# Attention and gated FFN on one core: small steps of the down product moved ahead of the attention's steps in each queue, one operand pair regrouped, bias, weight forms and loads at other places

## The reference

```python
x = x + attn(layernorm(x), ...)   # latent attention, causal, RoPE, width 64 after two projections
x = x + ffn(layernorm(x), W1, W2, W3)
# ffn: hidden = silu(x @ W1.T) * (x @ W3.T)      hidden width 2048
#      hidden = fwht(hidden)                     Walsh-Hadamard transform over 2048
#      out    = hidden @ W2.T
# attn: c = (x @ W_to_kv.T) @ W_compress.T; layernorm; q, k, v from c; RoPE; softmax(q k / 8) v;
#       z = o @ W_comp2lat.T; out = z @ W_to_kv + z @ W_out_res.T + b_out_res
```

## Time and profile before

| what | value |
|---|---|
| three runs, median (lowest to highest) | 2144.19 us (2143.27 to 2144.85) |
| the profiled execution's own time | 2144.14 us |
| its span in the trace | 2142.1 us |
| PE / DVE / ACT / POOL busy | 2010.1 / 1525.1 / 1157.8 / 1066.0 us |
| instructions | 32782 |

### The profile page before, as it was taken

How to read it: one execution, slowest core, us unless ns; L and a number is a source line. 1 busy time by engine, 2 the same in 40 slices (tenths; PEclk the granted TensorE clock), 3 DMA queues, 4 the chain that set the end, 5 groups by cost and what they waited for, 6 DMA issues and landing times.

```text
span 2142.1 us, 32782 instructions
## 1 busy us (share of the span) xinstructions
PE 2010.1 (94%) x11862; PEld 1167.0 (54%) x11862; DVE 1525.1 (71%) x2626; ACT 1157.8 (54%) x1775; POOL 1066.0 (50%) x788
## 2 busy tenths in 40 slices
PE   6889899989999999999999999999999999999998
PEld 3534344455555656556555555556565555556665
DVE  7897978758777686776777677776768768653333
ACT  5866455455554655555555646556564555543343
POOL 2356732556356454554546544554644545454444
PEclk8999999999999999999999999999999999999999
DMA  8656346454463524735346434545347353373322
GB/s 328 222 193 228 123 143 164 153 156 138 121 155 125 188 88 142 173 108 164 115 116 171 148 123 123 138 138 163 113 126 178 100 163 113 100 168 125 119 96 89
DMA packets 267264, 312.57 MB, mean 146 GB/s; under 512 B 181344, under 2 KB 191712, under 8 KB 265312
## 3 DMA queue, kind: packets, MB, share of 16 engines
q1 hardware_dynamic: 267104, 310.48, 47.7%
HBM read 221.02 MB, written 47.19 MB: 125 GB/s over the span
## 4 chain that ended last, share of the span: by engine, by line
PE 52%; DVE 19%; ACT 10%; issue 9%; POOL 6%; DMA 3%; SPq 1%; ACTq 0%; DVEq 0%; POOLq 0%
PE PF L1115 10%; PE PF L1117 10%; PE PF L1116 10%; PE PD L1199 4%; PE PD L1200 4%; PE PD L1201 4%; DVE H L2240 2%; POOL ring L2502 2%; DVE XS L2208 2%; DMA WS<-wscr 1%; DVE W2S L2234 1%; DVE Pl L1987 1%; ACT H L1593 1%; PE XY L936 1%; ACT W2S L1572 1%
## 5 line engine op out<-in xcount | busy, mean ns | idle before, releaser
L1115 PE MATMUL PF<-XF,WS 128*128 128x512 f16 x1778 | 676.2, 380 | 25.8 <-ACT PF L1545 10.3
L1116 PE MATMUL PF<-XF,WS 128*128 128x512 f16 x1778 | 674.3, 379 | 0.0
L1117 PE MATMUL PF<-XF,WS 128*128 128x512 f16 x1778 | 674.1, 379 | 0.0
L1199 PE MATMUL PD<-W2S,H 128*128 128x256 f16 x1456 | 397.2, 273 | 33.5 <-ACT W2S L1601 14.8
L1201 PE MATMUL PD<-W2S,H 128*128 128x256 f16 x1456 | 397.1, 273 | 0.0
L1200 PE MATMUL PD<-W2S,H 128*128 128x256 f16 x1456 | 397.1, 273 | 0.0
L2572 POOL TENSOR_TENSOR ring<-ring,W2S 128x512 f32<-128x512 f32 x192 | 257.0, 1341 | 203.2 <-ACT W2S L1601 203.2
L1117 PEld LDWEIGHTS PF<-XF,WS 128*128 128x128 f16 x1778 | 174.0, 98 | 210.1 <-issue 0.7
L1115 PEld LDWEIGHTS PF<-XF,WS 128*128 128x128 f16 x1778 | 173.8, 98 | 193.0 <-issue 36.1
L2554 POOL TENSOR_TENSOR SH<-SH 128x512 f32<-128x512 f32 x112 | 162.2, 1448 | 196.0 <-DVE SH L2234 191.6
L1116 PEld LDWEIGHTS PF<-XF,WS 128*128 128x128 f16 x1778 | 174.3, 98 | 124.2 <-issue 4.8
(11 more groups left out here) (371 smaller groups left out, 3606.0 us busy)
## 6 DMA issues: line engine op xcount, KB each, us to landing
WS<-wscr SPq DMA_DIRECT2D x112, 896.0 KB, 4.9
W2S<-w2f SPq DMA_DIRECT2D x196, 256.0 KB, 2.7
ring<-x SPq DMA_DIRECT2D x56, 256.0 KB, 5.3
wscr<-WS SPq DMA_DIRECT2D x16, 896.0 KB, 4.2
out<-ring SPq DMA_DIRECT2D x56, 256.0 KB, 3.2
RAW<-w13t SPq DMA_DIRECT2D x16, 512.0 KB, 4.6
xraw<-xT SPq DMA_DIRECT2D x28, 256.0 KB, 4.1
XF<-w SPq DMA_DIRECT2D x13, 512.0 KB, 18.1
```

Of the source, the lines that this page charges most:

```text
L1115: pe.matmul(bank, wh, th, start=i < 2 and j == 0, stop=False, skip_group_check=True)
L1116: pe.matmul(bank, wh, tl, start=False, stop=False, skip_group_check=True)
L1117: m = pe.matmul(bank, wl, th, start=False, stop=j == 1, skip_group_check=True)
L1199: pe.matmul(o, th, wh, start=i in (P1, P2, P5) and tp == 0 and r == 0, stop=False, skip_group_check=True)
```

## The change

- `take_at` (ACT) and `add_at` (DVE) move one `fill` earlier: a unit that ends in step (k, j) is emptied ahead of `fill(k, j)` and no longer behind it. On DVE `fill(k, 5)` goes behind `hidden(k, 1)` and the addition, except where it holds a softmax low part (`low_at`).
- `SPLITS`: A12 is split alone (512 wide, ACT and DVE), early in the even block; A22 is split with S4 (1024 wide, ACT at the end of the even block, POOL at the head of the odd one). Their places and counts change with it, and DVE's `parts_low` loses a wait.
- `bias`: row t at slot `tile_slot(a, t) + 4`, with no wait for V.
- `TPREP`: two of W2's sums in stage 0 and six in stage 1 (four and four before), at other steps.
- cproj's first half is at slot 3 for a >= 3 (2 before); the load of WS for block 1 of a stage is at j = 1 (2 before), ahead of the load of form 6.

```diff
--- before.py
+++ after.py
@@ -73,15 +73,15 @@
 ADDED = (6, 7, 8, 9, 12, 13)
 HFORM = ("A11", "S2", "S3", "A22", "A12", "S1", "S4")
-PLACE_A = {"A11": (0, 0), "S3": (1, 8), "S1": (2, 3), "S2": (4, 4), "A12": (5, 6), "A22": (7, 7), "S4": (16, 17)}
-PLACE_B = {"A11": 9, "S3": 10, "S1": 11, "S2": 12, "A12": 13, "A22": 14, "S4": 15}
-
-SPLITS = (("A11", "S3"), ("S1", "S2"), ("A12", "A22"), ("S4",))
+PLACE_A = {"A11": (0, 0), "S3": (1, 8), "S1": (2, 3), "S2": (4, 4), "A12": (16, 17), "A22": (7, 7), "S4": (5, 6)}
+PLACE_B = {"A11": 9, "S3": 10, "S1": 11, "S2": 12, "A12": 15, "A22": 14, "S4": 13}
+
+SPLITS = (("A11", "S3"), ("S1", "S2"), ("A12",), ("S4", "A22"))
 SPLIT_OF = {f: i for i, fs in enumerate(SPLITS) for f in fs}
 WFILE = (4, 0, 1, 2, 5, 3, 6)
-TPREP = ({33: 0, 42: 1, 51: 2, 60: 3}, {8: 4, 22: 5, 36: 6, 50: 7})
+TPREP = ({48: 0, 59: 1}, {8: 2, 18: 3, 28: 4, 38: 5, 48: 6, 58: 7})
 SPLIT_AT = {13 + i: i for i in range(16)}
@@ -91,7 +91,7 @@
-FORMS_AT = {0: 2, 6: 2}
+FORMS_AT = {0: 1, 6: 2}
 SUMS_AT = 11
@@ -173,6 +173,12 @@
     return None if q < QF or q >= NK // 4 - 1 else (q, 7 * (k % 4) + j)
+def low_at(k, j):
+
+    s, h = divmod(k, NH)
+    return s > 0 and any(slot == tile_slot(c, t) + 2 for c, slot in slots(s, 7 * h + j) for t in range(4))
+
+
 def done_at(k, j):
     v = half_at(k, j - 1) if j else half_at(k - 1, 6)
@@ -199,12 +205,12 @@
 def high_no(p, i):
-    return 16 + 4 * (p - 2 * QF) + i + 1
+    return 16 + 4 * (p - 2 * QF) + {0: 1, 2: 2, 1: 3, 3: 4}[i]
 def low_no(p, i):
-    return 2 * (p - 2 * QF) + {0: 1, 3: 2, 1: 17, 2: 18}[i]
+    return 2 * (p - 2 * QF) + {0: 1, 3: 2, 2: 17, 1: 18}[i]
 def sum_no(p, i):
@@ -501,7 +507,7 @@
         def parts_from(p, i):
-            return (SH[:, :, :], SH[:, :, :], SHO[:, :, :], SHO[:, 0, :])[i]
+            return (SH[:, :, :], SH[:, :, :], SHO[:, 0, :], SHO[:, :, :])[i]
         def parts_free(p, i):
@@ -677,8 +683,8 @@
                 q, r = x // 2, x % 2
                 w.wait_ge(d_w2st[q % 2], 224)
-                if x in (0, 4):
-                    w.wait_ge(v_xf, xf_no(x // 4, 6))
+                if x in (0, 2):
+                    w.wait_ge(v_xf, xf_no(x // 2, 6))
                 else:
                     w.wait_ge(d_tst, 16 * x)
                 sp.dma_start(TP, w2scr[q][:, r * 2048:(r + 1) * 2048]).then_inc(d_tld, 16)
@@ -948,8 +954,8 @@
                 yfree = (v_x2, tile_no(a, t))
             def attention(a, slot):
-                if slot in (2, 5):
-                    for k in (0, 1) if slot == 2 else (2, 3):
+                if slot in (2 if a < PLAIN else 3, 5):
+                    for k in (2, 3) if slot == 5 else (0, 1):
                         if a < PLAIN:
                             cproj1(a, k)
                         else:
@@ -1780,57 +1786,55 @@
                     high(k - 1)
                 if k == 4 * QF + 4:
                     parts_high(k // 2 - 1, 0)
-                take_at(k, 0)
+                if k > 4 * QF + 1 and k % 2 == 0:
+                    parts_high(k // 2 - 1, 2)
+                take_at(k, 1)
                 fill(k, 0)
                 if k:
                     copy_p5(k)
                 if k == 1:
                     tokens_high(0, 6)
-                if k > 4 * QF + 2 and k % 2:
-                    parts_high((k - 3) // 2, 3)
-                take_at(k, 1)
+                take_at(k, 2)
                 fill(k, 1)
                 if k > 4 * QF + 1 and k % 2 == 0:
                     parts_high(k // 2 - 1, 1)
                 if k > 4 * QF and k % 2 and k != 4 * QF + 3:
                     parts_high(k // 2, 0)
-                take_at(k, 2)
-                if k > 4 * QF + 1 and k % 2 == 0:
-                    parts_high(k // 2 - 1, 2)
                 if split and k > 1:
                     forms_high(h + 1, 0)
                     forms_high(h + 1, 1)
+                take_at(k, 3)
                 fill(k, 2)
                 if k:
                     silu(k, 0)
-                take_at(k, 3)
+                take_at(k, 4)
                 fill(k, 3)
                 if k == 1:
                     forms_high(2, 0)
                     forms_high(2, 1)
-                take_at(k, 4)
+                take_at(k, 5)
                 fill(k, 4)
                 if k == 0:
                     norms(15, 0)
                 silu(k, 1)
-                take_at(k, 5)
+                take_at(k, 6)
                 fill(k, 5)
+                if k > 4 * QF + 1 and k % 2 == 0:
+                    parts_high(k // 2 - 1, 3)
                 if k == 0:
                     norms(15, 1)
                     norms(13, 0)
                     norms(13, 1)
                     tokens_high(0, 2)
                     norms(14, 0)
-                take_at(k, 6)
                 if k % 4 < 3:
                     fill(k, 6)
+            parts_high(NK // 2 - 1, 2)
             parts_high(NK // 2 - 1, 1)
             take(NK // 4 - 1, 0)
-            parts_high(NK // 2 - 1, 2)
             take(NK // 4 - 1, 1)
-            take(NK // 4 - 1, 2)
             parts_high(NK // 2 - 1, 3)
-            for u in COPIED[3:]:
+            for u in COPIED[2:]:
                 take(NK // 4 - 1, u)
@@ -2027,7 +2031,7 @@
                 w.wait_ge(v_xf, xf_no(a // 2 - 1, 6))
                 if a in (2, 4):
-                    w.wait_ge(d_tst, 32 * a)
+                    w.wait_ge(d_tst, 16 * (2, 8)[a // 2 - 1])
                 ve.tensor_scalar(XS[:, a % 2, t, :], xrow(a, t), st[:, 184 + 2 * t:185 + 2 * t], st[:, 84 + t:85 + t],
                                  ALU.subtract, ALU.mult).then_inc(v_xs, 1)
@@ -2236,7 +2240,6 @@
             def parts_low(p, i):
                 w.wait_ge(a_hi, high_no(p, i))
-                w.wait_ge(g_S, sum_no(p, 2))
                 ve.tensor_tensor(parts_at(p, i, 1), parts_from(p, i), parts_at(p, i, 0), ALU.subtract).then_inc(v_lo, 1)
             def add_unit(q, u):
@@ -2439,6 +2442,7 @@
                 s, h = divmod(k, NH)
                 if k > 1:
                     hidden(k - 1, 0)
+                    add_at(k, 0)
                     fill(k - 1, 6)
                 if k == 0:
                     hidden(0, 0)
@@ -2449,24 +2453,22 @@
                     tokens_low(0, 2)
                     tokens_low(0, 4)
                     tokens_sum(0, 6)
-                add_at(k, 0)
                 fill(k, 0)
                 if k and k <= 4 * QF:
                     low_part(k - 1)
-                add_at(k, 1)
+                if k > 4 * QF + 1 and k % 2 == 0:
+                    parts_low(k // 2 - 1, 2)
+                add_at(k, 2)
                 fill(k, 1)
                 if k:
                     sum_c(k)
                     out_rows((k - 1) // 4 - 1, 2 * ((k - 1) % 4) + 1)
                 if k > 4 * QF + 1 and k % 2 == 0:
                     parts_low(k // 2 - 1, 1)
-                add_at(k, 2)
                 fill(k, 2)
-                if k > 4 * QF + 1 and k % 2 == 0:
-                    parts_low(k // 2 - 1, 2)
                 if k and s == 0 and h < NH - 1:
                     forms_low(h + 1, 0)
-                add_at(k, 3)
+                add_at(k, 4)
                 fill(k, 3)
                 if k:
                     sum_e(k)
@@ -2474,19 +2476,21 @@
                     tokens_low(0, 6)
                 if k and s == 0 and h < NH - 1:
                     forms_low(h + 1, 1)
-                add_at(k, 4)
+                add_at(k, 5)
                 fill(k, 4)
                 out_rows(k // 4 - 1, 2 * (k % 4))
-                add_at(k, 5)
+                if low_at(k, 5):
+                    fill(k, 5)
                 hidden(k, 1)
-                fill(k, 5)
                 add_at(k, 6)
+                if not low_at(k, 5):
+                    fill(k, 5)
                 if k == 0:
                     fill(k, 6)
             hidden(NK - 1, 0)
             add_at(NK, 0)
+            parts_low(NK // 2 - 1, 2)
             parts_low(NK // 2 - 1, 1)
-            parts_low(NK // 2 - 1, 2)
             for u in ADDED:
                 add_unit(NK // 4 - 1, u)
@@ -2589,9 +2593,9 @@
                     row_add(*before)
                 if k > 4 * QF and k % 2:
                     if j == 0:
+                        if k > 4 * QF + 2:
+                            parts_low((k - 3) // 2, 3)
                         form_sum(k // 2, 0)
-                    if j == 1 and k > 4 * QF + 2:
-                        parts_low((k - 3) // 2, 3)
                     if j == 3 and k != 4 * QF + 3:
                         parts_low(k // 2, 0)
                 if k > 4 * QF + 1 and k % 2 == 0:
@@ -2600,14 +2604,13 @@
                             parts_low(k // 2 - 1, 0)
                         form_sum(k // 2 - 1, 1)
                         form_sum(k // 2 - 1, 2)
-                    if j == 3:
+                    if j == 2:
                         form_sum(k // 2 - 1, 3)
             def attention(a, slot):
-                if slot in (12, 13):
-
```

(5 more changed lines are left out.)

## The result

| | before | after |
|---|---|---|
| median of the runs (lowest to highest) | 2144.24 us (2143.27 to 2144.85), 4 runs | 2153.56 us (2152.15 to 2155.15), 4 runs |
| ratio | | 1.0044, 95% interval 1.0027 to 1.0061 |
| the profiled execution's own time | 2144.14 us | 2155.15 us |
| its span | 2142.1 us | 2153.4 us |

The account below looks back on a forecast made before the run. PE, busy 2010.1 of 2142.1 us, was taken as the bound, its largest waits for ACT's takes and DVE's additions. Gains and losses summed to 22.9 us, giving 2121 us from 2144; own range 2111 to 2131, 8-in-10 range 2102 to 2141.

Parts of the forecast that it names:

- Step 1: Takes at (9,1) and (9,5), six stages: takes done in time and the wait for `hidden` gone, +17.8 us.
- Step 11: Exps behind a take at (3,2), (4,1), (5,0), (9,2), (12,5): start 0.6 to 0.7 us later, net 0, bounds +2 and -4.
- Step 4: (14,2) and (15,3), six stages: sum_c earlier only by work taken off DVE, +6.6 us, bounds 0 and 12.8.
- Step 10: Latent copies behind the take at (1,2) and (7,2): PE 1.5 us late, eleven times, -17 us, bounds 0 and -22.
- Step 2: Step (3,1), five stages: addition, `hidden` and Q waits go, some 0.8 us come back; +7 us, bounds 0 and 11.
- Step 5: copy_b, six stages: 0.85 us gained each at (12,2), 0.3 lost each at (13,2); +3.3 us.
- Steps 7 and 8: cproj at slot 3 delays form 6 at (0,5) and (0,6), -4.3 us; WS lands some 4 us earlier, +4 us.
- Step 9: W2's sums: stage 0 gains 3.5 us (bounds -2 and +7), stage 1 loses 2 (bounds 0 and -5).
- The sign for 2138: Rival: DVE stays the bound, 2138 us, chance 0.20; shown by L922 and sum_c waits as large as the units lost.
- the rival to which I gave 0.07: The change doesn't do what it says: the next wait in line takes each gain, 2143 us, chance 0.07.
- The one that ends slower (copy_b): 1024-wide split ending every even block makes copy_b the bound of product 2; 2174 us, chance 0.09.
- The rule that I weighed: DVE instructions with two SBUF inputs and GpSimd ones reading SBUF shut each other out; DVE's relief could be worth nothing.

Follow-up runs that it names:

- after_old_split: Changed kernel with the old split groups (A12 with A22, S4 alone) at their old places; 2152.61 us, ratio 1.0031 to the kernel before.
- after_split_behind_keys: Changed kernel with ACT's split of A22 and S4 one fill later, behind the low part of K; 2162.72 us, ratio 1.0089 to the kernel before.
- best4: best2 with the take behind the fill also at the steps that hold an exp; 2131.83 us, ratio 0.9943 to the kernel before.
- after_sum_c_first: Changed kernel with DVE's addition at j = 2 behind sum_c, no longer ahead of fill 1; 2152.45 us, ratio 1.0039 to the kernel before.
- after_old_bias: Changed kernel with POOL's four bias rows back at slots 12 and 13, behind the wait for V; 2176.01 us, ratio 1.0147 to the kernel before.
- before_bias: Kernel before with only the bias changed: row t at slot tile_slot + 4, no wait for V; 2132.22 us, ratio 0.9940.
- best2: best1 with W2's sums of stage 1 at steps 6, 15, 24, 33, 48 and 58; 2126.82 us, ratio 0.9921 to the kernel before.
- bias_takes_sums: Kernel before with new bias rows, copies and additions ahead of fills, take behind latent copy, W2's sums two in stage 0, six in stage 1; 2115.97 us.
- after_sum5_earlier: Changed kernel with sum 5 of stage 1 beginning at step 36 instead of 38; 2147.37 us, ratio 1.0017 to the kernel before.
- best1: Changed kernel with the take behind the latent copy at (1,2) and (7,2), sum 5 at step 36, DVE's j = 2 addition behind sum_c; 2130.92 us.

## Why the prediction was wrong

Point by point; the sizes are from the stalls by step, stage 4 for all of stages 2 to 6 unless said.

- **Step 1** (takes at (9,1) and (9,5), +17.8) failed, and it is the largest single error inside the stages, about 3.5 us in each. The takes went, but 3.1 us of stalls at (9,1) and (9,5) became 1.35 at (9,1), 1.43 at (9,6) and 0.8 to 1.14 at (10,1): worse than nothing. I counted K's low part ready 0.4 us before PE asks. It is 1.25 us late, since the 1.06 us split of A22 and S4 stands ahead of it on ACT, which I charged at (3,1) in step 2 and forgot at (9,1); after_old_split and after_split_behind_keys, which take it away, both leave 0.3 or less there.
- **Step 11** (exps behind a take, 0) failed in its place (9,2): sum_e at (9,6), as best4 shows. That taking it away costs as much elsewhere leaves its net size open.
- **Step 4** (+6.6) failed: 2.4 us became 3.0, -3.6. DVE is as full as I said, but with the new groups an addition and the 512-wide split both stand ahead of sum_c; taking either away (after_sum_c_first, after_old_split) brings (14,4) from 1.5 to 0.3. My lower bound of 0 was no bound, since I hadn't asked what moves in front.
- **Step 10** (latents, -17) was right: 11 x 1.5 = 16.5 in the trace, 13.2 and 15.6 us in two experiments.
- **Step 2** was right within an us: (3,1) gained 1.2 in each of five stages, 6 us for 7 (in stage 1 it lost 1.1). **Step 12** had 0 where stage 7 and the tail gained 1.2. **Step 5** had its two sizes right, 0.86 at (12,2) and 0.22 lost at (13,2), and missed the 0.40 that (12,3) gained. **Step 3** was too low: (2,2) gained 0.9 and (8,2) 0.3. **Steps 7 and 8** cancel nearly, as I had it, in stages 4 to 6 (2.3 us of stalls became 2.0); in stages 2 and 3 form 6 cost 2 us more, most of it at half the clock behind the wait. What step 8 had wrong is that form 6's low part is issued after WS has landed: in stage 3 it is issued at 903.54 and WS lands at 905.33. **Step 6** (+4) failed: (10,1) got a wait of ACT's part that it hadn't.
- **Step 9**: stage 0 gained 5.3, inside its bounds. Stage 1, to which I gave -2 with -5 as its worst, lost 12.8 in all; sum 5 alone accounts for the 8.9 of (6,4) and (6,5), of which some 2.3 are matmuls at half the clock (below). I had priced the sums by their work, and never asked where their loads stand in SP's queue.
- **A term that wasn't there**: the bias rows. They are one line of the change, and stand in my steps only behind the 0.56 us at (9,1) and among POOL's collisions in steps 4 and 6. Alone they are worth 12.7 us. Some of what I credited to the takes was theirs (takes' waits 21.4 to 11.9 with the bias alone). Without them the changed kernel is 31 us slower than the one before (after_old_bias), so the rest of the change was further from my sum than the result shows: without this gain, which my sum hardly had, the miss of 33 us would have been 55. That is luck.

Of the signs that I had named, takes without waits outside the tail, 11 waits for the latent copy (1.27 us idle each), waits for XF and none for WS came; waits for V at (2,2) did not grow to 1 us but fell to 0.2. The sign for 2138, waits at sum_c and the scores as large as what the units lost, came as well: sum_c has 17.9 us and the scores 14.9, where they had 0.2 and 4.1 before. The experiments put the scores' part down to ACT's split and not to DVE. Inside stages 2 to 6 the rival to which I gave 0.07, that the next wait takes each gain, is nearest to what was measured. The one that ends slower (copy_b) did not happen in the change and did in after_split_behind_keys. My own range, 2111 to 2131, does not come out of the bounds by any rule that I gave.

The rule that I weighed: the kernel before agrees with it, since DVE's 1024-wide split needs 2.31 us beside POOL's rows and 1.21 in before_bias without them. I had expected A22's move to POOL to relieve DVE by 0.5 us a pair. It did not: DVE is busy 1502.8 us with the old groups (after_old_split) and 1503.4 with the new ones, while POOL has 61.1 us more; the 21.7 us that DVE lost against the kernel before come from elsewhere in the change. Nor is DVE's fullest stretch any emptier; the window as long and as far into stage 3 as the second of the earlier trace rows has it busy for 20.06 of 20.40 us (19.98 before):

```profile
1115.50:1135.90 20.40, 19.06 (x119) 11.40 (x118) 20.06 (x36) 7.59 (x11) 7.16 (x5) 1.00 0.37 117
```

What stays open: how the 10.9 us between best2 and bias_takes_sums divide among the split groups, WS, cproj's place and the addition. On the changed kernel the groups alone were 1.0 us, the addition alone 1.1 and WS alone 2.4, all within the noise. cproj's place was never changed alone, and none of the four was changed alone with the other repairs in.

## What to carry to other kernels

In a kernel whose queues are full, a change of many parts is a sum of exchanges: time each part alone, because a good and a bad one hide each other (here -12.7 for the bias rows, -7.1 for the takes, -7.3 for the sums, against some +15 for the latent copies, +9 for one badly placed sum and +11 for the groups, the loads and the addition together). Moving an operation ahead of a point of the queue is free only where nothing behind it is due at that very step; list those steps and except them. And price a background task by the place of its load in the DMA queue and by what stands behind its wait on every engine, not by its busy time.

## What the runs showed of the hardware

**A wait can cost more than its length.** After PE's idle times of 1.91 and 4.39 us in stage 1 the granted clock is at half, its 1.2 GHz level, as the windows show (the eighth column is the clock):

```profile
476.00:484.00 8.00, 3.17 (x26) 1.92 (x23) 3.92 (x6) 3.37 (x4) 7.92 (x5) 1.00 0.54 201
...
484.00:486.00 2.00, 0.53 (x1) 0.50 (x2) 0.35 (x2) 1.99 (x5) 0.22 (x1) 0.50 0.00 0
486.00:488.00 2.00, 2.00 (x6) 0.63 (x5) 1.82 (x3) 0.41 (x1) 0.00 (x0) 0.50 0.00 0
488.00:490.00 2.00, 2.00 (x8) 1.01 (x7) 0.00 (x0) 0.69 (x1) 0.00 (x0) 0.50 0.00 0
```

Matmuls of 128x512 start 0.43 us apart there instead of 0.22; the 12 matmuls of (6,5) take 2.0 us more by it. In after_sum5_earlier, without those waits, the clock stays at 1.00 from 470 to 490 us. One wait of some 2 us can be enough. In stage 3 PE idles 2.12 us for form 6 until 907.34, and in stage 4 1.66 us until 1160.71; the windows behind them:

```profile
908.00:910.00 2.00, 2.00 (x6) 0.73 (x5) 0.50 (x1) 0.00 (x0) 0.00 (x0) 0.50 0.96 336
...
1161.00:1163.00 2.00, 2.00 (x14) 1.31 (x13) 1.34 (x2) 0.00 (x0) 0.13 (x1) 1.00 0.94 302
```

It isn't so each time: in after_sum5_earlier waits as long as the first, in stages 2 and 3, left the matmuls behind them at their usual spacing.

**A tiny operation on DVE can take as long as POOL's.** DVE and POOL in before_bias:

```profile
1029.77 2.05 DVE L1855 TENSOR_SCALAR st<-st 128x4 int32<-128x4 int32 x1
1031.73 0.16 DVE L1856 TENSOR_SCALAR st<-st 128x4 f32<-128x4 f32 x1
...
1029.66 2.13 POOL L2559 TENSOR_TENSOR H<-SH,H 128x1024 f16<-128x1024 f32 x1
```

Four elements a partition took 2.05 us beside a POOL split and 0.16 right behind it. The Trainium skill (SBUF — State Buffer, Who interferes with whom) has `tensor_scalar` among the operations that can, with operands that meet its conditions, take the port pair that DVE shares with GpSimd. It also says that the one that issues first blocks the other fully. The row agrees: POOL had begun 0.11 us earlier, and the two end within 0.03 us.

**Transfers delay each other's landing**: transposes that land 2.3 us after their issue took 4.7 behind a load of 512 KB (best1), and 3.1 became 5.9 to 6.4 behind one of 896 KB in six stages of the kernel after.
